# Causal mask added in the maximum, normalisation on ScalarE, and a new plan of the order, in a two-layer transformer block on one core

## The chip, the cores and the metric

The kernel runs on one core of one Trainium2 chip. The metric is the time of the program on the device in microseconds (us); lower is better. A core has five engines that each run their own instructions in order and meet through semaphores: TensorE (PE, matrix products into the banks of PSUM), VectorE (DVE), ScalarE (ACT), GpSimd (POOL) and SyncE (SP), which here issues all DMAs.

## The reference

The input is x of shape (8, 1024, 256), float32: 8 batches of 1024 tokens. Four blocks are applied, each on a layer normalisation of x and added to x:

```
x = x + attention0(norm(x))      16 heads of 16, causal softmax, w_qkv, w_out
x = x + ffn0(norm(x))            entmax-1.5 gates of 16 experts, factored 257 -> 128 -> 1024, exact gelu, back
x = x + attention1(norm(x))      16 heads, projections through a latent of 64, half of each head rotated, causal
x = x + ffn1(norm(x))            squared relu 256 -> 128 -> 256, and routed experts weighted by trunc(prob)
```

norm(x) is (x - mean) / sqrt(var + 1e-5) over 256. In the attentions score[q, k] for k > q is set to minus infinity before the softmax.

## The kernel before

Tokens are worked in halves of a batch, c = 0 or 1, of 512 tokens. `PASSES` (L73 to L80) is the order of the 32 attention passes (batch b, layer l, half c); for each batch from 1 on it is (b, 0, 1), (b-1, 1, 1), (b, 1, 0), (b+1, 0, 0). A pass has four units of four heads (`UNITS`, 128 in all; pass (4, 0, 1) begins with unit 64).

For each unit scores are formed twice. First query by key ("s" items, `score`, L1020): one matmul for each tile of 128 queries, head and part of up to 512 keys, into a ring of three PSUM banks. Where the part ends on the diagonal (2048 of 3072 tiles), a second matmul, identity by `mask_b`, adds -1e30 above the diagonal (L1029). VectorE reduces each tile to its row maximum (`maximum`, L1570). When a unit is through, the maxima are split in three bf16 parts ("mx"), transposed ("mt") and sent by DMA as rows under the queries ("mT"). Then the scores are formed key by query ("st", `scores_t`, L1039, two banks), with the maxima subtracted by those rows; ScalarE takes the exponential (L1336), GpSimd zeroes what lies above the diagonal in the probabilities (`causal`, L1484), and TensorE multiplies them with the values ("pv", L1064, an item for the four heads of a key tile). ScalarE copies the result out ("o"), TensorE transposes it and VectorE divides by the sums ("nm").

Beside the passes run side chains of items. A normalisation (L88) is: statistics on VectorE, the power -1/2 of the variance on GpSimd ("rstd", `inverse_root`, L1453), (x - mean) * rstd on VectorE in two steps of two instructions of 256 columns ("norm", `normalised`, L1537, which waits for GpSimd), and two transposes ("xt"). A projection (L93) has four products "qk" of two matmul pairs each, which ScalarE copies; in layer 1 they are rotated (VectorE "rot", "add", with GpSimd); ScalarE and GpSimd split each in three bf16 parts ("rest", "p1", "p2", GpSimd L1476 and L1481), SP stores the parts (`store_parts`, L842), and later SP loads a unit's stack of queries and keys from there ("ld", `load_stack`, L855, six DMAs). Then come values ("v"). `first_ffn` and `second_ffn` are the other chains.

The order of all items is one list, `ORDER`, made by `program_order` (L397) before the program is built; every engine walks the same list and takes its own items, SP and GpSimd too, so each queue is in the list's order. The planner `Plan` keeps a clock for PE, one busy time for each other engine (`on`, L208, which adds a hop of 0.2 us), and durations in `TIMES` (L145). At each step it lists what could run on PE, each with a time and a rank, and takes the lowest rank among those that can run now, or the earliest. Scores of a unit are "late" (rank 5, else 7) by a line that runs `LEAD` = 7.0 us ahead. `windows` (L172) gives, for every one or two passes, two lists of side steps: chain 0 (outputs and ffn) and chain 1 (loads and projections). They are handed over when the window's first pass begins. Chain 1 has an empty list beside pass (b, 0, 1), `first + ahead` (projections (b, 1, 0) and (b+1, 0, 0)) beside (b-1, 1, 1), and `second` (projections (b+1, 0, 1), then (b, 1, 1)) beside (b, 1, 0) and (b+1, 0, 0). A side chain is "due" (rank 4, else 8) when it lags behind the share of the window that has passed.

## Time and profile before

| | |
|---|---|
| median of 3 runs | 3432.05 us (3427.19 to 3440.59) |
| the profiled execution | 3424.19 us, its span 3422.5 us |
| busy: PE, DVE, ACT, POOL | 3100.3 (91%), 2443.0 (71%), 1927.9 (56%), 1070.7 us (31%) |
| granted clock of TensorE, mean | 0.974 of full speed |
| bytes moved by DMA | 268.54 MB, mean 78 GB/s |

A busy time counts an engine's time once, however many instructions overlap in it; matmuls do overlap, so the duration of one is longer than the time it takes of PE. The granted clock is the share of 2.4 GHz; 0.5 would be its lower level of 1.2 GHz. Durations, waits and chain all come from one execution.

### The profile page before, as it was taken

To read this page: it belongs to the slowest core of one execution; us is meant where nothing else is said; L and a number is where in the kernel's file an instruction comes from. 1 tells how busy PE (TensorE), PEld (TensorE's weight loads), DVE (VectorE), ACT (ScalarE), POOL (GpSimd) and SP (SyncE) were. 2 spreads that over 40 slices of the span, in tenths; PEclk is the share of its full clock that TensorE was granted. 3 is DMA by queue.
4 is the path that set the end of the run, shared out by engine and by line. 5 is a ranking of instruction groups with operands and counts; after the bars stand their busy time and mean duration, and the time that the engine had idled before them with its cause. 6 is when DMAs were issued, how large, how long until landed. Compare 5 with 4: busy or idle time off the path is not lost.

```text
span 3422.5 us, 59720 instructions
## 1 busy us (share of the span) xinstructions
PE 3100.3 (91%) x19319; PEld 1476.2 (43%) x19319; DVE 2443.0 (71%) x6387; ACT 1927.9 (56%) x4092; POOL 1070.7 (31%) x2476
## 2 busy tenths in 40 slices
PE   5899899998999989999899898999989999899997
PEld 3444444444444444434444354444544445344443
DVE  4776686857777577866778567785777847777683
ACT  2456555565465655656556565556655566455654
POOL 2225421345123441324313243132521325213321
PEclk8999999999999999999999999999999999999998
DMA  5415232235222451234413243232442325322240
GB/s 153 105 47 123 65 74 53 65 92 129 50 46 76 107 119 34 58 80 108 102 39 90 56 105 91 56 76 64 108 94 46 81 63 126 66 61 60 57 98 14
DMA packets 241216, 268.54 MB, mean 78 GB/s; under 512 B 19568, under 2 KB 208912, under 8 KB 240912
## 3 DMA queue, kind: packets, MB, share of 16 engines
q1 hardware_dynamic: 240912, 264.66, 32.5%
q8 instruction: 170, 2.79, 0.4%
q14 instruction: 134, 1.10, 0.1%
HBM read 162.35 MB, written 100.66 MB: 77 GB/s over the span
## 4 chain that ended last, share of the span: by engine, by line
PE 60%; DVE 19%; ACT 7%; DMA 6%; issue 4%; SPq 3%; POOL 1%; ACTq 0%; POOLq 0%; DVEq 0%
PE ps L1064 12%; PE ps L1027 10%; PE ps L1047 10%; DVE mx L1573 10%; PE ps L1001 6%; PE ps L993 5%; ACT probs L1336 4%; DMA stk_k<-k 4%; PE ps L1136 3%; PE ps L1131 3%; PE ps L1029 2%; PE ps L1123 2%; PE ps L981 1%; PE ps L1101 1%; DMA stk_q<-mT 1%
## 5 line engine op out<-in xcount | busy, mean ns | idle before, releaser
L1573 DVE TENSOR_REDUCE mx<-ps 128x1 f32<-128x512 f32 (+3 forms) x3072 | 1533.0, 549 | 503.9 <-PE ps L1029 353.5
L1336 ACT ACTIVATE probs<-ps 128x512 f32<-128x512 f32 (+3 forms) x3072 | 1382.2, 491 | 840.9 <-PE ps L1047 820.2
L1490 POOL TENSOR_SCALAR_AFFINE_SELECT probs<-probs 128x128 f32<-128x128 f32 x2048 | 604.9, 305 | 1763.8 <-ACT probs L1336 1734.7
L1027 PE MATMUL ps<-stk_k,stk_q 112*128 112x512 bf16 (+3 forms) x3072 | 882.2, 332 | 124.5 <-DVE mx L1573 69.1
L1047 PE MATMUL ps<-stk_q,stk_k 115*128 115x512 bf16 (+3 forms) x3072 | 893.1, 334 | 78.3 <-ACT probs L1336 47.8
L1064 PE MATMUL ps<-probs,vaug 128*17 128x512 f32 (+3 forms) x6144 | 629.3, 501 | 12.6 <-ACT probs L1336 6.8
L1047 PEld LDWEIGHTS ps<-stk_q,stk_k 115*128 115x128 bf16 x3072 | 273.5, 99 | 604.1 <-ACT probs L1336 419.0
L1027 PEld LDWEIGHTS ps<-stk_k,stk_q 112*128 112x128 bf16 x3072 | 296.1, 98 | 505.9 <-issue 337.5
L1029 PE MATMUL ps<-mask_b,ident_b 128*128 128x128 bf16 x2048 | 440.2, 222 | 0.0
L993 PE MATMUL ps<-turned,wqkv 128*128 128x512 f32 x512 | 265.7, 619 | 3.4 <-ACT turned L1286 1.6
L1029 PEld LDWEIGHTS ps<-mask_b,ident_b 128*128 128x128 bf16 x2048 | 201.5, 98 | 124.8 <-issue 39.6
L1476 POOL TENSOR_TENSOR scratch<-scratch,parts 128x512 f32<-128x512 f32 x128 | 148.1, 1157 | 285.9 <-ACT scratch L1303 264.6
L1064 PEld LDWEIGHTS ps<-probs,vaug 128*17 128x17 f32 x6144 | 121.9, 96 | 244.9 <-issue 109.4
L1286 ACT ACTIVATE turned<-ps 128x512 f32<-128x512 f32 x192 | 112.1, 601 | 127.9 <-PE ps L981 82.7
L1610 DVE TENSOR_TENSOR x<-ps,x 128x512 f32<-128x512 f32 x128 | 88.1, 688 | 126.2 <-PE ps L1001 125.3
L1481 POOL TENSOR_TENSOR parts<-scratch,parts 128x512 bf16<-128x512 f32 x128 | 149.7, 1170 | 46.0 <-ACT parts L1315 46.0
L1351 ACT ACTIVATE scratch<-ps 128x512 f32<-128x512 f32 x128 | 76.4, 597 | 152.5 <-PE ps L1131 152.3
L1131 PE MATMUL ps<-scratch,wout1T 128*128 128x512 f32 x256 | 135.8, 612 | 12.9 <-ACT scratch L1351 12.9
L1001 PE MATMUL ps<-wo,turned 128*128 128x256 f32 x512 | 139.5, 400 | 6.9 <-ACT turned L1286 6.8
L1001 PE MATMUL ps<-wqkv,turned 128*128 128x256 f32 x512 | 135.8, 389 | 0.1
L1136 PE MATMUL ps<-scratch,win 128*128 128x512 f32 x256 | 131.2, 594 | 0.0
L1546 DVE TENSOR_SCALAR xn<-x,mv,rstd 128x256 f32<-128x256 f32 x256 | 98.0, 425 | 40.2 <-POOL rstd L1456 40.2
(145 smaller groups left out, 2646.2 us busy)
## 6 DMA issues: line engine op xcount, KB each, us to landing
k<-parts SPq DMA_DIRECT2D x128, 384.0 KB, 3.4
stk_q<-q SPq DMA_DIRECT2D x256, 192.0 KB, 4.1
stk_k<-k SPq DMA_DIRECT2D x128, 384.0 KB, 6.0
q<-parts SPq DMA_DIRECT2D x64, 384.0 KB, 2.9
stk_k<-k SPq DMA_DIRECT2D x128, 192.0 KB, 4.3
x<-in_L_attn_x SPq DMA_DIRECT2D x16, 512.0 KB, 4.2
k<-parts SPq DMA_DIRECT2D x64, 128.0 KB, 3.4
stk_q<-q SPq DMA_DIRECT2D x128, 64.0 KB, 6.7
```

The costliest lines, as they stand in the source:

```text
L993: ins = pe.matmul(pt, wqkv[l][:, kd, D * w + P * m:D * w + P * (m + 1)], xT(2 * l, b, c, kd), start=kd == 0, stop=kd == KD - 1)
L1001: ins = pe.matmul(pt[:, D * i:D * (i + 1)], left(kd)[:, cols], right(kd), start=kd == 0, stop=kd == n_k - 1)
L1027: ins = pe.matmul(out, q, stk_k[0:ROWS_S, slot, h, BANK * p:BANK * p + width], start=True, stop=not diagonal)
L1029: ins = pe.matmul(out[:, width - P:width], ident_b[:], mask_b[:], start=False, stop=True)
L1047: pe.matmul(st_bank[n % len(ST_BANKS)][:, cols], stk_k[0:ROWS, slot, h, P * j:P * (j + 1)], stk_q[0:ROWS, slot, h, cols], start=True, stop ...
L1064: ins = pe.matmul(o_bank[32 * h:32 * h + DH + 1, cols], vaug[:, v, j % TPC, HG * g + h, :], probs[:, STEP[u, j] % PBUF, h, cols], start=j ...
L1131: pe.matmul(pt, wout1T[:, P * o:P * (o + 1)], z1, start=True, stop=True).then_inc(done, 1)
L1136: pe.matmul(acc, win2[:, k, :], hsb[k % 3], start=k == 0, stop=k == OC - 1)\
L1336: act.activation(probs[:, step % PBUF, h, cols], st_bank[n % len(ST_BANKS)][:, cols], ACT.Exp, scale=SCALE)\
L1481: pool.tensor_tensor(parts[:, o % PRING, 2], qf[o % QRING], parts[:, o % PRING, 1], ALU.subtract)\
L1490: pool.affine_select(out=diag, in_=diag, compare_op=ALU.is_ge, fill=0.0, base=0, pattern=[[1, P]], channel_multiplier=-1).then_inc(p_ready, 1)
L1573: dve.tensor_reduce(mx[:, h, i - TPC * c, p:p + 1], s_bank[n % len(S_BANKS)][:, 0:dict(score_parts(i))[p]], AX.X, ALU.max).then_inc(s_drai ...
```

## The change

- The second matmul of a diagonal tile is gone. VectorE's reduction of such a tile becomes one instruction that adds the last columns of a mask of 512 columns (zero but for the last 128), writes the tile back to PSUM and gives the maximum. The other 1024 tiles are reduced as before.
- "norm" goes from VectorE to ScalarE, as an activation with a per-partition scale (rstd) and bias (shift = -mean * rstd). VectorE computes -mean after the statistics, GpSimd the product after the power. ScalarE waits for it in its own order.
- The planner: other durations, overlap of neighbouring instructions, one transfer queue of all DMAs (`moving`), other ranks, LEAD 9. The waits for a free x slot and for free value slots become steps of the chains. A side chain that is empty takes the next window's list at once (`EARLY`). The ranks were pair 0, mt 1, nm 2, burst 3, due 4, late 5, st 6, s 7, chain 8, single 10 (pair and single are the value products of two key tiles or of one).

```diff
-LEAD = 7.0
+LEAD = 9.0
...
+    old = values_before(b, l, c)
+    if old:
+        steps.append(("after", ("pv", UNIT[old[0], old[1], NG - 1, old[2]], TT - 1)))
...
 def loaded(b, c):
-    return [([("load", b, c)], ""), ([("stat", b, c)], "")]
+    n = NC * b + c - X_SLOTS
+    before = [("after", ("out", n // NC, n % NC))] if n >= 0 else []
+    return before + [([("load", b, c)], ""), ([("stat", b, c)], "")]
...
-    "load": (0.0, ("SP", 6.0)), "stat": (0.0, ("DVE", 2.3)), "rstd": (0.0, ("POOL", 1.0)), "norm": (0.0, ("DVE", 0.9)),
...
-    "rot": (0.0, ("DVE", 1.6), ("POOL", 1.4)), "add": (0.0, ("DVE", 0.75)), "p0": (0.0, ("ACT", 0.6)),
-    "rest": (0.0, ("POOL", 1.25)), "p1": (0.0, ("ACT", 0.6)), "p2": (0.0, ("POOL", 1.25)),
...
-    "logit_": (0.5,), "logit": (0.5, ("DVE", 1.2)), "epow": (0.0, ("POOL", 1.0)), "ent": (0.0, ("DVE", 1.2)),
-    "eroot": (0.0, ("POOL", 1.0)), "at": (0.5, ("ACT", 0.6)), "g": (0.86, ("ACT", 0.6)), "h1_": (0.86,),
...
+    "load": (0.0, ("SP", 6.0)), "stat": (0.0, ("DVE", 2.2)), "rstd": (0.0, ("POOL", 1.35)), "norm": (0.0, ("ACT", 0.8)),
...
+    "rot": (0.0, ("DVE", 1.5), ("POOL", 1.0)), "add": (0.0, ("DVE", 0.68)), "p0": (0.0, ("ACT", 0.63)),
+    "rest": (0.0, ("POOL", 1.16)), "p1": (0.0, ("ACT", 0.63)), "p2": (0.0, ("POOL", 1.16)),
...
+    "logit_": (0.89,), "logit": (0.89, ("DVE", 1.7)), "epow": (0.0, ("POOL", 1.0)), "ent": (0.0, ("DVE", 1.6)),
+    "eroot": (0.0, ("POOL", 1.0)), "at": (0.44, ("ACT", 0.6)), "g": (1.05, ("ACT", 0.6)), "h1_": (0.86,),
...
-        self.busy[engine] = max(self.busy[engine], start) + time
-        return self.busy[engine] + HOP
+        begin = max(self.busy[engine], start)
+        self.busy[engine] = begin + time - OVERLAP[engine]
+        return begin + time + SEEN
+    def transfer(self, start, number, time):
+        begin = max(self.busy["SP"], start)
+        self.busy["SP"] = begin + 0.5 * number + 0.1
+        self.moving = max(self.moving, begin + 1.3) + time
+        return max(self.moving, begin + 1.5) + 0.3
...
-                self.parts[item[1:]] = self.on("SP", time, 1.2) + 2.5
+                self.parts[item[1:]] = self.transfer(time, 3.6 if item[5] else 1, 2.2 if item[5] == 0 else 5.3)
...
-            self.loads[u] = self.on("SP", start, 6 * 0.6) + 3.0
+            self.loads[u] = self.transfer(start, 6, 7.9 if UNITS[u][3] else 5.3)
...
+        self.pe = max(self.pe, self.score_time()) + width / 2400 + 0.003
-        self.pe = max(self.pe, self.score_time()) + width / 2300 + (0.09 if diagonal else 0.02)
-        end = self.on("DVE", self.pe + HOP, 0.12 + width / 1000)
+        end = self.on("DVE", self.pe + HOP, (0.2 if diagonal else 0.15) + width / 960)
...
-        self.rows[u] = self.on("SP", end, 0.6) + 2.2
+        self.rows[u] = self.transfer(end, 1.4, 0.1)
...
-        self.pe = max(self.pe, self.scores_t_time(u, j, h)) + (z - a) / 2300
-        end = self.on("ACT", self.pe + HOP, 0.04 + (z - a) / 1000)
+        self.pe = max(self.pe, self.scores_t_time(u, j, h)) + (z - a) / 2400 + 0.003
+        end = self.on("ACT", self.pe + HOP, 0.17 + (z - a) / 1200)
...
-            end = self.on("POOL", end, 0.32)
+            end = self.on("POOL", end, 0.29)
...
-        self.pe = start + 4 * (z - a) / 2400 + 0.2
+        self.pe = start + 4 * (z - a) / 2400 + 0.02 + (0.2 if alone else 0.1)
...
-        if todo and (not main or position >= window_end):
-            passes, *beside = todo.pop(0)
-            for n in range(2):
-                plan.chains[n] += beside[n]
-            for step in beside[1]:
-                if step[0] != "after" and step[0] and step[0][0][0] == "qk_" and step[1]:
-                    for w in range(2):
-                        plan.chains[2 + w] += splits(*step[0][0][1:4], w)
+        begin = todo and (not main or position >= window_end)
+        for n in range(2):
+            if todo and (begin or EARLY and not plan.chains[n]):
+                beside, todo[0][1 + n] = todo[0][1 + n], []
+                plan.chains[n] += beside
+                for step in beside:
+                    if step[0] != "after" and step[0] and step[0][0][0] == "qk_" and step[1]:
+                        for w in range(2):
+                            plan.chains[2 + w] += splits(*step[0][0][1:4], w)
+        if begin:
+            passes = todo.pop(0)[0]
...
+RANK = dict(mt=1, nm=2, burst=3, late=4, st=5, pair=5.5, due=6, s=7, chain=8, single=10)
+EARLY = True
...
-                diagonal = BANK * p + width == P * (i + 1)
                 q = stk_q[0:ROWS_S, slot, h, P * i - BANK * c:P * (i + 1) - BANK * c]
-                ins = pe.matmul(out, q, stk_k[0:ROWS_S, slot, h, BANK * p:BANK * p + width], start=True, stop=not diagonal)
-                if diagonal:
-                    ins = pe.matmul(out[:, width - P:width], ident_b[:], mask_b[:], start=False, stop=True)
-                ins.then_inc(s_full, 1)
+                pe.matmul(out, q, stk_k[0:ROWS_S, slot, h, BANK * p:BANK * p + width], start=True, stop=True).then_inc(s_full, 1)
...
+            def normalised(n, b, c, a):
+                i, src = NC * n + c, x[:, x_slot(b, c)]
+                if a == 0:
+                    act.wait_ge(ln_rstd, LN["rstd", n, b, c] + 1)
+                    if normed:
+                        bk, k = PLACE["xt", *normed[-1], KD - 1]
+                        act.wait_ge(full[bk], k + 1)
+                    normed.append((n, b, c))
+                for t in range(2 * a, 2 * a + 2):
+                    ins = act.activation(xn[:, t, :], src[:, t, :], ACT.Identity, bias=shift[:, i, t:t + 1], scale=rstd[:, i, t:t + 1])
+                ins.then_inc(xn_ready, 1)
...
-                pool.tensor_tensor(rstd[:, i], veps[:, i], neg_half[:], ALU.pow).then_inc(ln_rstd, 1)
+                pool.tensor_tensor(rstd[:, i], veps[:, i], neg_half[:], ALU.pow).then_inc(ln_root, 1)
+                pool.wait_ge(ln_root, LN["rstd", n, b, c] + 1)
+                pool.tensor_tensor(shift[:, i], minus[:, i], rstd[:, i], ALU.mult).then_inc(ln_rstd, 1)
...
+                dve.tensor_scalar(minus[:, i], mv[:, i, :, 0], -1.0, None, ALU.mult)
...
-                dve.tensor_reduce(mx[:, h, i - TPC * c, p:p + 1], s_bank[n % len(S_BANKS)][:, 0:dict(score_parts(i))[p]],
-                                  AX.X, ALU.max).then_inc(s_drained, 1)
+                width = dict(score_parts(i))[p]
+                tile, top = s_bank[n % len(S_BANKS)][:, 0:width], mx[:, h, i - TPC * c, p:p + 1]
+                if BANK * p + width == P * (i + 1):
+                    dve.tensor_tensor_reduce(tile, tile, mask_b[:, BANK - width:BANK], 1.0, LOWEST, ALU.add, ALU.max, top)\
+                        .then_inc(s_drained, 1)
+                else:
+                    dve.tensor_reduce(top, tile, AX.X, ALU.max).then_inc(s_drained, 1)
```

## Rows read from the trace of the kernel before

**Rows 1.** Page, part 1: busy us (share of span) xinstructions, by engine.
```profile
PE 3100.3 (91%) x19319; PEld 1476.2 (43%) x19319; DVE 2443.0 (71%) x6387; ACT 1927.9 (56%) x4092; POOL 1070.7 (31%) x2476
```

**Rows 2.** Page, part 4: chain that ended last, share of the span by engine, by line.
```profile
PE 60%; DVE 19%; ACT 7%; DMA 6%; issue 4%; SPq 3%; POOL 1%; ACTq 0%; POOLq 0%; DVEq 0%
PE ps L1064 12%; PE ps L1027 10%; PE ps L1047 10%; DVE mx L1573 10%; PE ps L1001 6%; PE ps L993 5%; ACT probs L1336 4%; DMA stk_k<-k 4%; PE ps L1136 3%; PE ps L1131 3%; PE ps L1029 2%; PE ps L1123 2%; PE ps L981 1%; PE ps L1101 1%; DMA stk_q<-mT 1%
```

**Rows 3.** Windows: us, busy us (xinstructions) of each engine, PEclk, DMA share, GB/s.
```profile
0.00:70.00 70.00, 34.53 (x170) 22.00 (x170) 28.12 (x42) 17.75 (x30) 12.88 (x22) 0.87 0.42 132
3360.00:3422.50 62.50, 39.47 (x184) 19.40 (x184) 10.65 (x37) 19.89 (x44) 6.84 (x22) 0.74 0.05 18
```

**Rows 4.** Waits of the whole run: who <- for whom: us, times, longest us.
```profile
DVE mx L1573 <- PE ps L1029: 353.5, 316, 8.8
...
PE ps L1027 <- DVE mx L1573: 69.1, 141, 2.6
...
PE ps L1047 <- ACT probs L1336: 47.8, 135, 1.2
...
PE ps L1027 <- DMA stk_k<-k: 45.9, 29, 3.9
...
PE ps L1047 <- DMA stk_q<-mT: 19.7, 7, 3.9
```

**Rows 5.** Windows, six stretches: the one at 2070, and all six summed.
```profile
2070.00:2110.00 40.00, 31.59 (x231) 13.41 (x223) 32.40 (x73) 17.35 (x41) 14.68 (x40) 0.91 0.64 138
...
sum 245.00, PE 196.93 PEld 84.60 DVE 196.60 ACT 109.78 POOL 93.70; mean PE 32.82 PEld 14.10 DVE 32.77 ACT 18.30 POOL 15.62
```

**Rows 6.** Chain of waits, 1625 to 1700: start us, us, what.
```profile
1649.45 1.14 POOL parts L1481
1650.60 0.56 SPq L852
...
1657.22 7.49 DMA stk_k<-k
...
1688.98 6.01 DMA stk_q<-mT
```

**Rows 7.** Timeline of TensorE: start us, us, engine, line, instruction.
```profile
1646.06 0.22 PE L1027 MATMUL ps<-stk_k,stk_q 112*128 112x128 bf16 x1
1646.12 0.22 PE L1029 MATMUL ps<-mask_b,ident_b 128*128 128x128 bf16 x1
1646.17 0.22 PE L1027 MATMUL ps<-stk_k,stk_q 112*128 112x128 bf16 x1
```

**Rows 8.** Page, part 5: group | busy us, mean ns | idle before, releaser.
```profile
L1573 DVE TENSOR_REDUCE mx<-ps 128x1 f32<-128x512 f32 (+3 forms) x3072 | 1533.0, 549 | 503.9 <-PE ps L1029 353.5
```

**Rows 9.** Groups by line and shape, VectorE: | busy us, mean ns | idle before.
```profile
L1573 DVE TENSOR_REDUCE mx<-ps 128x1 f32<-128x512 f32 x1536 | 1008.1, 682 | 241.1 <-PE ps L1027 136.7 <-PE ps L1029 98.3
...
L1610 DVE TENSOR_TENSOR x<-ps,x 128x512 f32<-128x512 f32 x128 | 88.1, 688 | 126.2 <-PE ps L1001 125.3
...
L1695 DVE SCALAR_TENSOR_TENSOR scratch<-ps,bias,scratch 128x512 f32<-128x512 f32 x32 | 24.0, 750 | 13.6 <-PE ps L1123 8.6 <-PE ps L1136 5.0
```

**Rows 10.** The same view, all engines: normalisation and the rows near its new form.
```profile
L1546 DVE TENSOR_SCALAR xn<-x,mv,rstd 128x256 f32<-128x256 f32 x256 | 98.0, 425 | 40.2 <-POOL rstd L1456 40.2
...
L1533 DVE TENSOR_SCALAR veps<-mv 128x4 f32<-128x4 f32 x64 | 11.5, 179 | 2.2
...
L1336 ACT ACTIVATE probs<-ps 128x512 f32<-128x512 f32 x1536 | 856.8, 598 | 417.3 <-PE ps L1047 409.6
...
L1336 ACT ACTIVATE probs<-ps 128x256 f32<-128x256 f32 x512 | 184.0, 383 | 137.6 <-PE ps L1047 131.4
...
L1315 ACT ACTIVATE parts<-scratch 128x512 bf16<-128x512 f32 x128 | 81.3, 635 | 25.1 <-POOL scratch L1476 25.1
...
L1490 POOL TENSOR_SCALAR_AFFINE_SELECT probs<-probs 128x128 f32<-128x128 f32 x2048 | 604.9, 305 | 1763.8 <-ACT probs L1336 1734.7
...
L1456 POOL TENSOR_TENSOR rstd<-veps,neg_half 128x4 f32<-128x4 f32 x64 | 64.6, 1009 | 63.6 <-DVE veps L1533 63.6
```

More of the change, by code:

```diff
@@ L82, with values_before @@
 UNIT = {key: u for u, key in enumerate(UNITS)}
+X_SLOTS = 5
+def values_before(b, l, c):
+    if c == l == 0:
+        return (b - 1, 0, 1) if b > 1 else None
+    if c == l:
+        return (b - 1, 1, 1) if b else (0, 0, 1)
+    if l:
+        return (b, 0, 1) if b else None
+    return (b - 2, 1, 1) if b > 1 else (0, 0, 1) if b else None
 def normalisation(n, b, c):
@@ L154 @@
-    "keep": (0.0,), "route_": (0.5,), "route": (0.5, ("DVE", 0.9)), "up_": (0.86,), "up": (0.86, ("ACT", 0.6), ("DVE", 0.8)),
-    "gate": (0.0, ("ACT", 0.3), ("DVE", 1.3)), "down": (0.9, ("DVE", 0.7)), "out": (0.0,),
-}
+    "load": (0.0, ("SP", 6.0)), "stat": (0.0, ("DVE", 2.2)), "rstd": (0.0, ("POOL", 1.35)), "norm": (0.0, ("ACT", 0.8)),
+    "xt": (0.44, ("ACT", 0.6)), "yt": (0.44, ("ACT", 0.6)), "qk_": (0.86,), "qk": (0.86, ("ACT", 0.9)),
+    "rot": (0.0, ("DVE", 1.5), ("POOL", 1.0)), "add": (0.0, ("DVE", 0.68)), "p0": (0.0, ("ACT", 0.63)),
@@ new lines @@
+    "rest": (0.0, ("POOL", 1.16)), "p1": (0.0, ("ACT", 0.63)), "p2": (0.0, ("POOL", 1.16)),
+    "v_": (0.86,), "v": (0.86, ("ACT", 0.6)), "ao_": (0.86,), "ao": (0.86, ("DVE", 1.9)),
+    "logit_": (0.89,), "logit": (0.89, ("DVE", 1.7)), "epow": (0.0, ("POOL", 1.0)), "ent": (0.0, ("DVE", 1.6)),
+    "eroot": (0.0, ("POOL", 1.0)), "at": (0.44, ("ACT", 0.6)), "g": (1.05, ("ACT", 0.6)), "h1_": (0.86,),
+    "h1": (0.86, ("DVE", 0.75)), "hid": (0.86, ("ACT", 0.6)), "z": (0.86,), "fo": (0.86, ("DVE", 1.9)),
@@ L157 @@
+    "keep": (0.0,), "route_": (0.89,), "route": (0.89, ("DVE", 1.1)), "up_": (0.86,), "up": (0.86, ("ACT", 0.6), ("DVE", 0.75)),
+    "gate": (0.0, ("ACT", 0.3), ("DVE", 1.6)), "down": (0.86, ("DVE", 0.7)), "out": (0.0,),
+}
+OVERLAP = {"ACT": 0.1, "DVE": 0.08, "POOL": 0.0, "SP": 0.0}
+SEEN = 0.06
 HOP = 0.2
@@ L199, in __init__ @@
         self.free, self.turn, self.ring, self.st, self.steps, self.pvs, self.held = [0.0, 0.0], 0, [], [], {}, [], []
-        self.parts, self.rows, self.out = {}, {}, {}
+        self.parts, self.rows, self.out, self.moving = {}, {}, {}, 0.0
         self.s_unit, self.s_items, self.waiting, self.outputs, self.s_first, self.loads = 0, score_items(0), [], [], {}, {}
@@ L359, in weigh_pair, with weigh @@
     def weigh_pair(self):
-        self.weigh()
-        self.weigh()
-    def weigh(self):
+        self.weigh(False)
+        self.weigh(False)
+    def weigh(self, alone=True):
         u, j = self.held[0]
@@ L404, in program_order @@
         total += DENSE * unit_work(u)
-    todo = windows()
+    todo = [list(window) for window in windows()]
     window_end = 0
@@ L476, in program_order @@
                 if time < NEVER:
-                    choices.append((time, 3 if burst else 4 if due else 8, "chain", (n,)))
+                    choices.append((time, RANK['burst'] if burst else RANK['due'] if due else RANK['chain'], "chain", (n,)))
         time = plan.score_time()
         if time is not None:
-            choices.append((time, 5 if late(plan.s_unit, len(plan.s_items)) > 0 else 7, plan.score, ()))
+            choices.append((time, RANK['late'] if late(plan.s_unit, len(plan.s_items)) > 0 else RANK['s'], plan.score, ()))
         if main and "gelu" not in plan.locks and position < window_end:
@@ L483, in program_order @@
             if time is not None:
-                choices.append((time, 6, "st", main[0]))
+                choices.append((time, RANK['st'], "st", main[0]))
         if not choices:
```

47 lines of the change are left out of this document (13 added, 34 removed).

## The prediction

> **What bounds the kernel now.** I read the page's busy shares first: TensorE (PE) 3100.3 of 3422.5 us, and in the table VectorE (DVE) at 2443.0, ScalarE (ACT) at 1927.9, GpSimd (POOL) at 1070.7 [rows 1]. The reader is to see one engine nearly full and a second at seven tenths. Next the chain that ended last: 60% of it is PE, 19% DVE, 7% ACT, 9% transfers and their issue (DMA 6%, SPq 3%), 4% issue [rows 2]. So an edit on PE is worth most of what it takes away, one on DVE about a quarter: 19% of 3422.5 is 650 us of chain on 2443 us of busy time, or 27%.
>
> Then PE's idle time, 3422.5 - 3100.3 = 322 us. Start (0 to 70) and end (3360 on) hold 59 of it, in which no edit does much: 70 - 34.53 = 35.5, and 62.5 - 39.47 = 23 [rows 3]. Of the rest the list of waits names 69.1 us behind VectorE's maxima, 47.8 behind exponentials, and 45.9 and 19.7 behind the transfers of a stack and of the row maxima [rows 4]. These transfer waits are not spread out. Six stretches of 40 to 45 us, one per batch, hold a hole in PE: the one shown has 31.59 busy of 40 at a granted clock of 0.91 in place of 1.00, and all six 196.9 of 245, so 48 us idle [rows 5]. The chain through the one at 1650 tells why: the split of a projection on POOL ends at 1650.6, only then SP sends its stores (L852) and, behind them in its in-order queue, the load of the next stack; that takes 7.49 us; then the row maxima take 6.01 us more, and PE has transposed scores again at 1688.98 + 6.01 = 1695.0 [rows 6]. That the load stands behind these stores follows from the order of items: unit 64's "ld" comes after the "p2" of (3, 1, 1, 0, 1). The planner had written that load 3.6 us of SP and 3.0 us of landing, and the projection's split at times of its own.
>
> **The change, part by part.** All sums are made against the profiled execution (3424.2 us, span 3422.5). The median of the runs shown is 3432.05, so I add 8 us at the end.
>
> (A) Mask off TensorE. 2048 matmuls of 128 columns and their weight loads go. A row says 219 ns for one, but that is a latency. What one takes of PE's time is start to start, from the mask to the next score: 1646.12 to 1646.17, and 0.06 from the score to the mask where the score has as many columns, so 0.06 us [rows 7]; 2048 x 0.06 = 123 us. That is the upper bound (PE counts everywhere). The lower is the share of line L1029 in the chain, 2% or 68 us [rows 2]. I take 85: above the chain's share because a score tile also reaches DVE a step earlier, and DVE's longest wait is for L1029 (353.5 us) [rows 4]. Saved: **85 (68 to 123)**.
>
> (B) Mask on VectorE. In the 2048 diagonal tiles of the 3072, a reduction becomes add, maximum and a write of the tile back to PSUM. No row shows this instruction. At width 512 the reduction takes 682 ns, a tensor-tensor add with one operand in PSUM 688, a three-operand one out of PSUM 750 [rows 9]. So +6 to +68 ns, 12 to 139 us of DVE. If the maximum is delivered by a small instruction of its own, a row of 4 elements of 179 ns [rows 10] bounds it: 367 us. I take +0.05, 102 us, near the upper of the two 512-wide rows, since this one must both write the tile and deliver a value. L1573 is 10% of the chain [rows 2], 342 us, on 1533 us busy [rows 8], so 22% of it is on the path: 102 x 0.22 = 22 us. Lost: **22 (3 to 81)**. A doubling is a rival below. DVE also loses the reason to wait for the second matmul.
>
> (C) Normalisation on ScalarE. DVE gives up 256 instructions of 425 ns, 98.0 us of work [rows 10], and gets 64 small ones of 179 ns, 11.5 us. ScalarE gets 256 of 256 columns. Its rows: 383 ns for 256 columns out of PSUM, 635 for 512 from SBUF [rows 10]; those are the ends, 98 to 163 us. The slope (598 - 383)/256 = 0.84 ns taken off the SBUF row gives 0.42 us, so 108 us. POOL gets 64 products of 4 columns between 305 ns (its mask of the probabilities) and 1009 (its power), 20 to 65 us, and each normalisation starts that much later [rows 10]. On the path: DVE gives back 86 x 0.27 = 23; ACT, whose 7% of the chain is 240 us on 1928 busy (12%), takes 108 x 0.12 = 13; the later start costs between nothing and all 65, and I put it at 5, since POOL has 1% of the chain [rows 2]. Saved: **5 (-62 to +11)**; the ends are 23 - 20 - 65 and 23 - 12. Queued behind the new wait on ScalarE are the exponentials; behind the old one on DVE were the maxima.
> The Trainium skill (ScalarE: Activation LUTs, section What ACT_TABLE_LOAD costs) puts 186 ns + 0.833 ns per element on an activation with immediates and about 93 more for each per-partition operand, of which there are two here: 585 ns, 150 us in all. By it ScalarE would take 18 us of path in place of 13. No row here has such an operand.
>
> (D) The hole per batch. Three edits aim at it. The planner now carries one transfer queue with 7.9 us for a stack of the second half. LEAD goes from 7 to 9, so scores run further ahead. And an empty side chain takes its next window's steps at once: beside pass (b, 0, 1) the second chain's list is empty in every batch from 1 on, so the projections for layer 1 and the next batch can start there, a window before they do now, and the splits on POOL are done before the stack load stands behind their stores. If they work, the six holes give 48 us and the clock up to 9% of 245, 22: 70 at most. What is late next is DVE, 32.40 of 40 busy there already [rows 5], and it must do the same maxima. I take **40 (0 to 70)**.
>
> (E) The rest of the order. 322 - 59 - 48 = 215 us of PE idle remain, of which 69.1 + 47.8 are waits for DVE and ACT of 0.35 to 0.5 us in the mean (47.8/135, 69.1/141) [rows 4], the size of the corrections in the new table (0.02 to 0.5 us an item). The ranks change too: pairs of value products no longer go first, side chains that are due go behind scores. It can cut either way: two thirds of the 117 named, or half the 69 on top. I take **20 (-35 to +80)**.
>
> Sum: -85 + 22 - 5 - 40 - 20 = -128; 3424 - 128 = 3296, plus 8: 3304, rounded to **3300 us**.
>
> **The rivals.**
> 1. The order pays fully (chance 0.15). PE becomes the only bound: 123 of (A), 70 of (D), 60 of (E), less 22 for (B) and 20 of new waits on ScalarE: 3424 - 211 + 8 = about 3220. For it: 215 us of idle are in waits that a true model can see. Against it: where PE is short of work now DVE is at 80% [rows 5], and no order removes maxima.
> 2. The order gives nothing (0.17): (D) and (E) at zero, because the holes only move to another place or the early projections compete with work that was ready. Then 3424 - 68 + 8 = 3364. For it: the load is in SP's queue behind stores whatever the planner believes, and POOL runs 93.7 us of the 245 there [rows 5].
> 3. ScalarE's new wait gives the gain back (0.08), the case on the other side. The place is the first of two normalising steps: ScalarE stands in order until POOL has power and product (1.0 + 0.3 to 1.0 us) and then works 4 x 0.42 = 1.7 us, while two banks of transposed scores cover 2 x 0.6 = 1.2 us. If it always arrives too early, PE loses up to 2.5 us for each of 64 normalisations, 160 us: 3296 + 160 + 8 = 3464. It decides from 2 us per normalisation (128/64). For it: PE waits for the exponentials in 135 places already [rows 4]. Against it: DVE, which had this wait, stood in it 40.2 us in all [rows 10].
> 4. VectorE's new instruction runs at half rate (0.05). The reduction's time per element is (682 - 549)/(512 - 384) = 1.04 ns, 384 being the mean width of all 3072 [rows 8, 9]; once more of it is 333 ns at the diagonal tiles' mean width of 320, 681 us of DVE: 2443 - 86 + 681 = 3038 us, over PE's 2977. At the 0.91 that the fullest engine now reaches this is 3340; if a second pass takes the whole of a 688 ns add (0.49 us at width 320, 1000 us), 3357/0.91 = 3690. It decides from 0.37 us per tile (3424 x 0.91 = 3116, less 2357, over 2048).
> The Trainium skill (Vector Engine (DVE) Microarchitecture Reference, section 7, Points that are easy to get wrong) says that such a form with two non-bf16 SBUF sources runs at half throughput. By that rule it would be the 3340, but here one source is in PSUM and the mask is bf16.
>
> **How the numbers follow.** Forecast 0.55, with its own range 3255 to 3345. The terms' bounds give 3432 - 123 + 3 - 11 - 70 - 80 = 3151 and 3432 - 68 + 81 + 62 + 35 = 3542, which don't meet in one run. Leaving out about one in ten on each side, with rival 1 inside and rival 2 inside: **3215 to 3390**. A measurement of this kernel can tell about 0.5%, 17 us. Faster: 0.55 + 0.15 + 0.17 and half of rival 4 less what their edges lose, 0.86; within 0.5%: 0.05; slower: 0.09, from rivals 3 and 4.
>
> **What would show it.** (A) No row of the mask on PE, PE busy about 2980 to 3010. (B) The new DVE row at width 512 in 690 to 790 ns; above 1000, rival 4. (C) Normalising rows on ScalarE of 0.38 to 0.6 us; its wait for POOL under 60 us in all; over 120, rival 3. (D) In the list of waits, PE behind stack and row-maxima transfers down from 65.6 us to under 25; if it stays, rival 2. (E) PE idle under 270 us. The prediction is wrong if PE's busy share falls below 0.88: then the time sits in waits that I take for cured.

## The result and the profile after

The changed kernel takes 3278.31 us (median of 4 runs, 3268.96 to 3287.42) against 3429.62 of the kernel before, timed beside it: ratio 0.9558, 95% interval 0.9512 to 0.9604. Forecast were 3300 us and a range of 3215 to 3390. The profiled execution took 3268.96 us, span 3267.1, so 155 us less than before.

Page of the changed kernel, part 1, busy time by engine, to be laid beside [rows 1]:
```profile
PE 2958.2 (91%) x17271; PEld 1344.2 (41%) x17271; DVE 2447.2 (75%) x8243; ACT 2018.0 (62%) x4348; POOL 1082.0 (33%) x2540
```
TensorE's busy time fell by 142 us, its idle time only from 322 to 309. Part 4, the chain, beside [rows 2]:
```profile
PE 57%; DVE 22%; ACT 10%; issue 4%; DMA 3%; POOL 2%; SPq 2%; ACTq 0%; DVEq 0%; POOLq 0%
PE ps L1083 11%; PE ps L1066 11%; PE ps L1049 10%; PE ps L1024 6%; DVE ps L1599 6%; ACT probs L1369 5%; DVE mx L1602 4%; PE ps L1016 4%; PE ps L1155 3%; PE ps L1150 3%; ACT xn L1318 2%; PE ps L1004 2%; DMA stk_k<-k 1%; PE ps L1142 1%; PE ps L1091 1%
```
TensorE went from 60 to 57%, VectorE from 19 to 22%, ScalarE from 7 to 10%, transfers and SP from 9 to 5%. Waits (who <- for whom: us, times, longest), beside [rows 4]:
```profile
PE ps L1066 <- ACT probs L1369: 52.4, 136, 1.4
...
PE ps L1049 <- DVE mx L1599: 41.0, 95, 9.6
...
PE ps L1049 <- DVE mx L1602: 17.9, 72, 0.7
...
PE ps L1066 <- DMA stk_q<-mT: 13.1, 25, 1.1
```
```profile
PE ps L1049 <- DMA stk_k<-k: 2.1, 4, 0.7
```
The transfer waits of TensorE went from 65.6 to 15.2 us: the holes at the stack loads are gone. On these lines the waits for maxima (69.1 before, 58.9 now) and for exponentials (47.8, now 52.4) stayed. Summed over all lines of TensorE that wait for maxima they are 85.6 before and 94.3 now. The new instructions, groups by line and shape, beside [rows 9, 10]:
```profile
L1602 DVE TENSOR_REDUCE mx<-ps 128x1 f32<-128x512 f32 x1024 | 702.0, 686 | 112.9 <-PE ps L1049 109.0 <-DVE hq L1755 0.2
L1599 DVE CUSTOM_DVE_ANT_0 ps<-ps,mask_b 128x512 f32<-128x512 f32 x512 | 347.7, 699 | 111.4 <-PE ps L1049 109.5
L1599 DVE DVE_READ_ACCUMULATOR2_ANT mx<- 128x1 f32 x2048 | 286.4, 140 | 0.0
...
L1599 DVE CUSTOM_DVE_ANT_0 ps<-ps,mask_b 128x128 f32<-128x128 f32 x512 | 145.5, 303 | 42.1 <-PE ps L1049 41.2
```
```profile
L1318 ACT ACTIVATE xn<-x,shift,rstd 128x256 f32<-128x256 f32 x256 | 138.7, 598 | 56.3 <-POOL shift L1493 55.6
```
```profile
L1493 POOL TENSOR_TENSOR shift<-minus,rstd 128x4 f32<-128x4 f32 x64 | 12.9, 201 | 5.0
```
The masked maximum is two instructions, 699 ns at width 512 and 140 ns for the read of the accumulator. The timeline shows what the pair takes:
```profile
1569.92 0.73 DVE L1599 CUSTOM_DVE_ANT_0 ps<-ps,mask_b 128x512 f32<-128x512 f32 x1
1570.57 0.14 DVE L1599 DVE_READ_ACCUMULATOR2_ANT mx<- 128x1 f32 x1
1570.57 0.73 DVE L1599 CUSTOM_DVE_ANT_0 ps<-ps,mask_b 128x512 f32<-128x512 f32 x1
...
1571.22 0.73 DVE L1599 CUSTOM_DVE_ANT_0 ps<-ps,mask_b 128x512 f32<-128x512 f32 x1
```
Start to start it is 0.65 us, since the next instruction begins together with the read. The plain reduction of the same width, back to back, starts every 0.60 us in the trace of the kernel before. A normalising row on ScalarE takes 598 ns where I had put 420; the product on GpSimd takes 201 ns.

### The profile page after: what moved, and what is told of

It is laid out like the page before. It is cut to its first block, busy times and chain, and to the rows that moved or that the text cites. A ratio compares the mean times of both kernels' runs of the same rounds, so it can differ in the third digit from the quotient of the medians.

```text
span 3267.1 us, 57797 instructions
## 1 busy us (share of the span) xinstructions
PE 2958.2 (91%) x17271; PEld 1344.2 (41%) x17271; DVE 2447.2 (75%) x8243; ACT 2018.0 (62%) x4348; POOL 1082.0 (33%) x2540
## 4 chain that ended last, share of the span: by engine, by line
PE 57%; DVE 22%; ACT 10%; issue 4%; DMA 3%; POOL 2%; SPq 2%; ACTq 0%; DVEq 0%; POOLq 0%
PE ps L1083 11%; PE ps L1066 11%; PE ps L1049 10%; PE ps L1024 6%; DVE ps L1599 6%; ACT probs L1369 5%; DVE mx L1602 4%; PE ps L1016 4%; PE ps L1155 3%; PE ps L1150 3%; ACT xn L1318 2%; PE ps L1004 2%; DMA stk_k<-k 1%; PE ps L1142 1%; PE ps L1091 1%
## 5 line engine op out<-in xcount | busy, mean ns | idle before, releaser
L1599 DVE CUSTOM_DVE_ANT_0 ps<-ps,mask_b 128x512 f32<-128x512 f32 (+3 forms) x2048 | 978.0, 503 | 278.6 <-PE ps L1049 271.7
L1066 PE MATMUL ps<-stk_q,stk_k 115*128 115x512 bf16 (+3 forms) x3072 | 876.8, 331 | 82.5 <-ACT probs L1369 52.4
L1049 PE MATMUL ps<-stk_k,stk_q 112*128 112x512 bf16 (+3 forms) x3072 | 845.0, 330 | 80.3 <-DVE mx L1599 41.0
L1602 DVE TENSOR_REDUCE mx<-ps 128x1 f32<-128x512 f32 x1024 | 702.0, 686 | 112.9 <-PE ps L1049 109.0
L1083 PE MATMUL ps<-probs,vaug 128*17 128x512 f32 (+3 forms) x6144 | 615.8, 493 | 19.4 <-POOL probs L1527 10.3
L1049 PEld LDWEIGHTS ps<-stk_k,stk_q 112*128 112x128 bf16 x3072 | 287.0, 98 | 567.9 <-issue 452.2
L1599 DVE DVE_READ_ACCUMULATOR2_ANT mx<- 128x1 f32 x2048 | 286.4, 140 | 0.0
L1318 ACT ACTIVATE xn<-x,shift,rstd 128x256 f32<-128x256 f32 x256 | 138.7, 598 | 56.3 <-POOL shift L1493 55.6
L1630 DVE RECIPROCAL rec<-ps 128x16 f32<-128x16 f32 x128 | 32.9, 257 | 172.4 <-PE ps L1091 162.1
```

Of the source, the lines that this page charges most:

```text
L1049: pe.matmul(out, q, stk_k[0:ROWS_S, slot, h, BANK * p:BANK * p + width], start=True, stop=True).then_inc(s_full, 1)
L1066: pe.matmul(st_bank[n % len(ST_BANKS)][:, cols], stk_k[0:ROWS, slot, h, P * j:P * (j + 1)], stk_q[0:ROWS, slot, h, cols], start=True, stop ...
L1083: ins = pe.matmul(o_bank[32 * h:32 * h + DH + 1, cols], vaug[:, v, j % TPC, HG * g + h, :], probs[:, STEP[u, j] % PBUF, h, cols], start=j ...
L1318: ins = act.activation(xn[:, t, :], src[:, t, :], ACT.Identity, bias=shift[:, i, t:t + 1], scale=rstd[:, i, t:t + 1])
L1599: dve.tensor_tensor_reduce(tile, tile, mask_b[:, BANK - width:BANK], 1.0, LOWEST, ALU.add, ALU.max, top)\
L1602: dve.tensor_reduce(top, tile, AX.X, ALU.max).then_inc(s_drained, 1)
```

## The experiments

Ratios are to the kernel before, timed beside each run, with their 95% intervals. Differences in microseconds are differences of ratios times 3430; one against the changed kernel carries its interval, 16 us to either side, and those of the others besides. First the three parts, one by one: mask (M), normalisation (N), order (O).

**M alone, and M without VectorE's price.** The first run has the mask's part of the change and nothing else; `ORDER` is the old one, item for item. The second leaves the mask out of these scores altogether:

```diff
-                if diagonal:
-                    ins = pe.matmul(out[:, width - P:width], ident_b[:], mask_b[:], start=False, stop=True)
...
+                    dve.tensor_tensor_reduce(tile, tile, mask_b[:, BANK - width:BANK], 1.0, LOWEST, ALU.add, ALU.max, top)\
+                        .then_inc(s_drained, 1)
```
and for the second, on top of it:
```diff
-                if BANK * p + width == P * (i + 1):
-                    dve.tensor_tensor_reduce(tile, tile, mask_b[:, BANK - width:BANK], 1.0, LOWEST, ALU.add, ALU.max, top)\
-                        .then_inc(s_drained, 1)
-                else:
-                    dve.tensor_reduce(top, tile, AX.X, ALU.max).then_inc(s_drained, 1)
+                dve.tensor_reduce(top, tile, AX.X, ALU.max).then_inc(s_drained, 1)
```

> Only the mask is moved from TensorE to VectorE's maximum; normalisation stays on VectorE, and the order of items is the old one, item for item. Theory A (steps A and B of the prediction: 85 us saved, 22 lost): ratio to before 0.982, some 3368 us; PE busy down by 120 to 140 us, but PE idle up by 60, because the old order leaves PE waiting for VectorE. Rival (most of the whole gain is this edit, since in the trace of after TensorE's busy time fell by 142 us and its idle time by only 13): ratio 0.965, some 3310 us, PE idle up by less than 20 us.

> The old order and normalisation on VectorE, and no mask in the query-by-key scores at all: the mask matmuls are gone and VectorE reduces every tile as before, so the row maxima are taken over the whole diagonal tile. They are then upper bounds of the causal maxima; any bound gives the same softmax, and the probabilities above the diagonal are still zeroed by GpSimd. So it is the mask-only run less VectorE's extra work. Theory (VectorE's add and accumulator read, 71 us of busy time there, took back what TensorE saved): ratio to before 0.975 to 0.982, 50 to 75 us better than the mask-only run. Rival (in the old order TensorE's mask time lay beside waits anyway): within 15 us of the mask-only run, ratio 0.993 or more.

Measured: M alone 3422.65 us, ratio 0.9976 (0.9962 to 0.9990). Without VectorE's price 3408.68 us, 0.9927 (0.9906 to 0.9948). In microseconds that is 8 and 25: in the old order VectorE's add cost 17, and taking the mask matmuls off TensorE, 123 us by the prediction's estimate, was worth 25. The first run fell outside both its theories; of their signs only the idle time (up by 60 foretold, 55 measured) held. In the second the theory fell and the rival was all but met: 14 us by the medians and 17 by the ratios, where it said 15, and 0.9927 where it said 0.993. Page, part 1, of M alone, then of the run without the mask:
```profile
PE 3041.6 (89%) x17271; PEld 1341.2 (39%) x17271; DVE 2514.1 (74%) x8435; ACT 1925.3 (56%) x4092; POOL 1070.2 (31%) x2476
```
```profile
PE 3044.8 (89%) x17271; PEld 1347.7 (40%) x17271; DVE 2440.9 (72%) x6387; ACT 1924.0 (56%) x4092; POOL 1071.2 (31%) x2476
```
In both TensorE's busy time falls by 56 to 59 us, not by 123, and its idle time, span less busy, rises from 322 to 377 and 367. Its waits in M alone:
```profile
PE ps L1032 <- DVE mx L1578: 65.7, 162, 3.0
PE ps L1049 <- ACT probs L1338: 54.6, 155, 1.4
PE ps L1032 <- DMA stk_k<-k: 49.5, 36, 3.2
PE ps L1032 <- DVE mx L1581: 31.7, 66, 1.6
```
Maxima 97.4 in place of 69.1, exponentials 54.6 for 47.8, the stack's transfer 49.5 for 45.9. TensorE comes sooner to the same waits. And its granted clock fell, from 0.974 to:
```profile
core 0: 3418.8 us, clock 0.965
```
On 3042 us of busy time that is 28 us at most. The start times of the matmuls close the account. In the kernel before, the step from a mask matmul to the next matmul is 0.058 or 0.059 us for over six in ten of the 2048 and longer for the rest; at 0.058 that makes 119 us in all. Of these, 55 came back as idle time. Busy time fell by only 59, so another 60 came back inside it: some 28 as a lower clock at most, the rest as longer steps from one matmul to the next. What they waited for no row tells. VectorE's 17 us are within these sums.

**N in the old order.** On top of M:

```diff
-                    ins = dve.tensor_scalar(xn[:, t, :], src[:, t, :], mv[:, i, t, 0:1], rstd[:, i, t:t + 1],
-                                            ALU.subtract, ALU.mult)
...
+                    ins = act.activation(xn[:, t, :], src[:, t, :], ACT.Identity, bias=shift[:, i, t:t + 1], scale=rstd[:, i, t:t + 1])
```

> Mask on VectorE and normalisation on ScalarE, with the old order. Theory (step C, 5 us saved): within 0.3% of the mask alone. Rival (ScalarE's 598 ns per normalising instruction and its wait for GpSimd delay exponentials in an order that was not planned for it): 0.5 to 1.5% slower than the mask alone, with ScalarE's wait for the shift over 60 us.

Measured: 3424.01 us, 0.9972 (0.9957 to 0.9987): no change against M alone. The theory (within 0.3% of M alone) stood and the rival fell; ScalarE waited 22.4 us for the shift, where the rival wanted over 60.

**O alone, and N and M in the new order.** The order of the changed kernel with the old work, then with N, with M, and (the changed kernel) with both. The first has the diff of the planner alone; the other two undo one part of the changed kernel:

```diff
-                    dve.tensor_tensor_reduce(tile, tile, mask_b[:, BANK - width:BANK], 1.0, LOWEST, ALU.add, ALU.max, top)\
...
+                    ins = pe.matmul(out[:, width - P:width], ident_b[:], mask_b[:, BANK - P:BANK], start=False, stop=True)
```
```diff
-                    ins = act.activation(xn[:, t, :], src[:, t, :], ACT.Identity, bias=shift[:, i, t:t + 1], scale=rstd[:, i, t:t + 1])
...
+                    ins = dve.tensor_scalar(xn[:, t, :], src[:, t, :], mv[:, i, t, 0:1], rstd[:, i, t:t + 1],
+                                            ALU.subtract, ALU.mult)
```

> The new order of items with the old work: mask matmuls on TensorE, normalisation on VectorE. Theory (steps D and E, 60 us saved): ratio to before 0.982. Rival 1 (the order only pays with the new work, for which its durations are made): ratio 1.00. Rival 2 (the holes at the stack loads are all that it cures): ratio 0.987, PE's idle time behind transfers of stack and row maxima under 25 us here too.

> The changed kernel with the mask matmuls back on TensorE (its order and its normalisation on ScalarE unchanged). Theory (TensorE's time is worth nearly all of itself in the new order, since its chain share of PE is still 57%): 85 to 123 us slower than the changed kernel less 22 given back by VectorE, so ratio to before 0.975 to 0.985. Rival (under the new order VectorE bounds and the mask is free on TensorE): ratio 0.960 or less.

> The changed kernel with normalisation back on VectorE, everything else and the order item for item the same: VectorE then has both the mask and the normalisation. Theory (VectorE's time has a price in the new order that it has not in the old: moving normalisation off it was worth 37 us there with the mask on TensorE): 37 to 60 us slower than the changed kernel, ratio to before 0.966 to 0.973. Rival (those 37 us were GpSimd's and ScalarE's timing, not VectorE's load, so they don't grow and the mask still pays its 43): 3310 to 3320 us, ratio 0.964 to 0.967. Second rival (VectorE overloaded, so the mask pays nothing without the other move): 3345 us or more, ratio 0.974 or more.

| | old order | new order |
|---|---|---|
| old work | 1 | 0.9782 (0.9759 to 0.9805) |
| N | not run | 0.9673 (0.9652 to 0.9694) |
| M | 0.9976 (0.9962 to 0.9990) | 0.9700 (0.9679 to 0.9721) |
| M and N | 0.9972 (0.9957 to 0.9987) | 0.9558 (0.9512 to 0.9604) |
| N, no mask in these scores | not run | 0.9503 (0.9478 to 0.9529) |

The medians were 3358.43 (order alone), 3321.38 (with N), 3328.28 us (with M). In microseconds the order alone gives 75, N on top of it 37, M on top of that 39; the other way round M 28 and then N 49. In the old order M and N together give 10. And taking the mask matmuls away with no price on VectorE is worth 58 us in the new order (0.9673 to 0.9503, normalisation on ScalarE in both), 25 in the old. The order alone came close to its theory (0.982) and far from rival 1. Rival 2 had the transfer waits right, 15.4 us with the old work too, but not the size, 0.987. With the mask back on TensorE the ratio, 0.9673, fell between its two cases, 0.975 and 0.960: the mask was worth 39 us, not the 63 to 101 of the theory. Part 1 of the mask back on TensorE, and of the changed kernel with normalisation back on VectorE:
```profile
PE 3056.7 (92%) x19319; PEld 1483.4 (45%) x19319; DVE 2378.9 (72%) x6195; ACT 2023.0 (61%) x4348; POOL 1081.6 (33%) x2540
```
```profile
PE 2997.2 (90%) x17271; PEld 1359.7 (41%) x17271; DVE 2517.8 (75%) x8435; ACT 1905.3 (57%) x4092; POOL 1072.1 (32%) x2476
```
From the first to the changed kernel busy falls by 98.5 us and idle rises by 43. The second was 49 us slower than the changed kernel, within the 37 to 60 of its theory, with 30% of the chain on VectorE where the changed kernel has 22%. But it does not show the theory's price. Its rival said that the 37 us would not grow, and 37 and 49 differ by less than their intervals. And 81 us less of VectorE, in the maxima, were worth only 19 in the same order (the run without the mask, below), or 23%; at that price the 71 us of normalisation would be worth 17. The contrast between 49 and 19 is not clear of noise either, since both are measured against the changed kernel. That the mask still pays 28 speaks against the second rival.

What stands beside it is another wait: TensorE's transposes (L1004) wait for the normalised rows. In order: the order alone, the old work with its own plan (below), the changed kernel with normalisation back on VectorE, the changed kernel:
```profile
PE ps L1004 <- DVE xn L1569: 36.1, 19, 4.7
```
```profile
PE ps L1004 <- DVE xn L1569: 15.3, 8, 4.7
```
```profile
PE ps L1004 <- DVE xn L1565: 40.1, 19, 4.7
```
```profile
PE ps L1004 <- ACT xn L1318: 18.1, 15, 5.7
```
With the mask on TensorE and normalisation on ScalarE it is 19.1 us; in the old order it is 15.4 with normalisation on VectorE and 14.9 on ScalarE, where the move was worth nothing. So 17 of the 37 us and 22 of the 49 lie in this wait, and it is long only where an order that was planned for normalisation on ScalarE runs it on VectorE. Maxima are the next part: summed over all lines, TensorE waits 81.4 us for them in the order alone and 66.1 with N, 117.1 and 94.3 in the other pair. The trace with normalisation back on VectorE is of an execution 16 us above the median of its kernel, so these differences are somewhat too large.

**What in the order.** Three runs of the changed kernel, each with one part of its planner taken back.

```diff
-EARLY = True
+EARLY = False
```
```diff
-RANK = dict(mt=1, nm=2, burst=3, late=4, st=5, pair=5.5, due=6, s=7, chain=8, single=10)
+RANK = dict(pair=0, mt=1, nm=2, burst=3, due=4, late=5, st=6, s=7, chain=8, single=10)
```
```diff
-            self.loads[u] = self.transfer(start, 6, 7.9 if UNITS[u][3] else 5.3)
+            self.loads[u] = self.on("SP", start, 6 * 0.6) + 3.0
...
```

The third takes back all durations, hops and the transfer queue.

> The changed kernel, planned with EARLY = False: a side chain gets its next list only when its window begins. Theory (the early start is what removes the stack-load holes, step D, 40 us): 30 to 50 us slower than the changed kernel, ratio to before 0.966 to 0.970, and PE's waits for the transfer of a stack back above 30 us. Rival (truer durations alone remove them): within 10 us of the changed kernel, ratio 0.958, those waits under 10 us.

> The changed kernel, planned with the old ranks (pairs of value products first, due side chains before late scores and transposed scores). Theory (step E, 20 us in all, ranks the larger part): 10 to 20 us slower than the changed kernel, ratio 0.960 to 0.963. Rival (ranks are the core of the order's gain, because VectorE's maxima are what PE must keep fed): 50 us or more slower, ratio 0.971 or more, with VectorE's wait for scores up by over 50 us.

> The changed kernel, planned with the old durations, hops and transfers, but with the new ranks, LEAD 9 and the early start. Theory (the transfer model is what sees the holes): 20 to 40 us slower than the changed kernel, ratio 0.963 to 0.969. Rival (durations hardly matter, the rules do): within 10 us, ratio under 0.959.

Measured: without the early start 3319.86 us, 0.9664 (0.9638 to 0.9689), 36 us worse than the changed kernel; old ranks 3376.87, 0.9838 (0.9814 to 0.9861), 96 worse; old durations 3328.97, 0.9689 (0.9667 to 0.9712), 45 worse. Together that is 177, more than the 142 that the whole new order gives on top of M and N (0.9972 to 0.9558). That the parts need each other is likely but not clear of noise, since the changed kernel's interval enters the first sum three times. LEAD and the chains' new waits for free slots had no run of their own. Waits for transfers, without the early start and then with the old durations:
```profile
PE ps L1049 <- DMA stk_k<-k: 7.2, 8, 4.2
...
PE ps L1066 <- DMA stk_q<-mT: 3.7, 7, 0.6
```
```profile
PE ps L1049 <- DMA stk_k<-k: 44.7, 25, 4.0
...
PE ps L1066 <- DMA stk_q<-mT: 20.3, 11, 3.5
```
and with the old ranks:
```profile
PE ps L1049 <- DMA stk_k<-k: 27.3, 15, 3.7
```
With 7.0 us for row maxima that is 34.3. The 65 us of transfer waits come back whole with the old durations, in part with the old ranks, and not without the early start (10.9). So the durations with the transfer queue closed the holes, with help of the ranks. For the early start the theory had the size and its rival the transfer waits; for the ranks the rival (50 us or more) stood; for the durations the ratio lay at the edge of the theory, 0.969. The early start earns its 36 us elsewhere. Where, the page of each run shows; without the early start, then with the old ranks:
```profile
PE 3005.9 (91%) x17271; PEld 1354.9 (41%) x17271; DVE 2449.3 (74%) x8243; ACT 2022.7 (61%) x4348; POOL 1080.9 (33%) x2540
```
```profile
PE 3048.7 (90%) x17271; PEld 1342.5 (40%) x17271; DVE 2422.7 (72%) x8243; ACT 2026.0 (60%) x4348; POOL 1083.9 (32%) x2540
```
The changed kernel and these two have the same 17271 matmuls, and yet TensorE is busy 2958, 3006 and 3049 us. Their granted clocks, 0.981, 0.972 and 0.969, explain 27 and 36 of the 48 and 91 us if all busy time goes with the mean clock. Split by the granted clock, TensorE's busy time at 2.4 GHz is 2861, 2852 and 2867 us in the three traces, and at 1.2 GHz 97, 154 and 182 us. So the extra busy time lies nearly all in stretches at the lower level. If all that is busy there is work at half rate, the lower clock explains half of what was added there, 29 and 42 us. This is an estimate; the rest, 19 and 48 us, are then longer steps from one matmul to the next, since the matmuls are the same. How a wait can hide there is argued: a row of 0.22 us of which 0.06 is its turn [rows 7] covers a wait of 0.16 behind it. What these steps waited for is not shown. Idle time differs little (309, 311 and 323 us), though waits move within it: without the early start TensorE waits 83.5 us for exponentials in place of 57.3, and 69.2 for maxima in place of 94.3. VectorE waits longer for scores in both, 377.7 us without the early start and 405.8 with the old ranks, where it was 271.7:
```profile
DVE ps L1599 <- PE ps L1049: 405.8, 319, 30.2
```

**The planner for the old work.**

```diff
-    "rstd": (0.0, ("POOL", 1.35)), "norm": (0.0, ("ACT", 0.8)),
+    "rstd": (0.0, ("POOL", 1.0)), "norm": (0.0, ("DVE", 0.8)),
...
-        self.pe = max(self.pe, self.score_time()) + width / 2400 + 0.003
-        end = self.on("DVE", self.pe + HOP, (0.2 if diagonal else 0.15) + width / 960)
+        self.pe = max(self.pe, self.score_time()) + width / 2400 + (0.06 if diagonal else 0.003)
+        end = self.on("DVE", self.pe + HOP, 0.15 + width / 960)
```

> The work of before (mask matmuls on TensorE, normalisation on VectorE) with the new planner, whose durations are set to that work: 0.06 us of PE per mask, 0.15 us + width/960 of VectorE for every maximum, normalisation 0.8 us on VectorE, power 1.0 us on GpSimd. Theory 1 (the order of the changed kernel was bad for the old work only because it was planned for other work): better than the order-only run by 15 us or more, ratio to before 0.974 or less. Theory 2 (the planner's rules carry the gain whatever the work): within 8 us of the order-only run, ratio 0.976 to 0.981.

Measured: 3340.64 us, 0.9730 (0.9709 to 0.9752), 18 us better than the order alone (3358.43). Theory 1 stands, a little above its 15 us (the intervals leave 7 to 29), and the wait for the normalised rows, 36.1 us in the order alone and 15.3 here, is 21 us shorter. Of the whole gain of 151 us 93 are then to be had with no change of the work, and mask and normalisation together are worth the other 59.

**Better than both.**

> The changed kernel without the mask in the query-by-key scores (maxima over the whole diagonal tile, one reduction of the old kind), with its order item for item. Theory (VectorE's 90 us of extra busy time at the 22% to 30% that VectorE has of the chain): 20 to 30 us better than the changed kernel, ratio to before 0.947 to 0.950. Rival (VectorE bounds in the scores' stretches): 50 us or more better, ratio under 0.941.

> The same work as the run before it (no mask in those scores, normalisation on ScalarE), with every maximum at 0.15 us + width/960 in the planner, and ranks, LEAD, PACE, DENSE and SPREAD set by a random search that minimised the planner's own finish. It finishes 95 us earlier by the planner's clock than with the ranks of the changed kernel. Theory (the planner's differences hold on the chip, as the 50 us for the early start came out as 41): 60 to 95 us better than the run before it, ratio to before 0.920 to 0.932. Rival (the search fits the planner's errors): less than 30 us better, ratio 0.940 or more.

The first is the edit shown above for the old order. The second's, in the planner alone:

```diff
-        end = self.on("DVE", self.pe + HOP, (0.2 if diagonal else 0.15) + width / 960)
+        end = self.on("DVE", self.pe + HOP, 0.15 + width / 960)
...
-LEAD = 9.0
-PACE = 0.9
-DENSE = 2.0
-SPREAD = 1.0
+LEAD = 14.9
+PACE = 0.64
+DENSE = 2.3
+SPREAD = 1.78
...
-RANK = dict(mt=1, nm=2, burst=3, late=4, st=5, pair=5.5, due=6, s=7, chain=8, single=10)
+RANK = dict(mt=0.0, nm=5.3, burst=0.7, late=4.4, st=3.7, pair=5.5, due=5.5, s=9.7, chain=6.3, single=10)
```

Measured: 3258.89 us, 0.9503 (0.9478 to 0.9529), and 3248.89 us, 0.9465 (0.9440 to 0.9491). The first is 19 us better than the changed kernel, just under the stated 20 to 30, on 81 us less of VectorE; its rival (50 or more) fell. The searched order gave 10 of the 95 us that the planner saw, so its rival (less than 30) stood; the intervals of the two overlap. Part 1 of the page and the clock, first of the run without the mask, then of the searched order:
```profile
PE 2959.0 (91%) x17271; PEld 1351.1 (41%) x17271; DVE 2365.9 (73%) x6195; ACT 2018.9 (62%) x4348; POOL 1084.8 (33%) x2540
```
```profile
core 0: 3256.6 us, clock 0.977
```
```profile
PE 2976.4 (92%) x17271; PEld 1359.4 (42%) x17271; DVE 2367.3 (73%) x6195; ACT 2014.8 (62%) x4348; POOL 1082.6 (33%) x2540
```
```profile
core 0: 3247.4 us, clock 0.964
```
Idle time fell from 298 to 271 us, but the granted clock from 0.977 to 0.964 of full speed, which on 2959 us of busy time is 39 us. Busy time at 1.2 GHz rose from 117 to 205 us, half of which rise is 44. Given back whole, these would bring the 10 us to 54 at most, still under the 60 to 95 foretold: the lower clock took a part, and the planner was too hopeful besides. How the two share it stays open. These two kernels rest on maxima over keys that the mask excludes; with scores much larger above the diagonal than below, exponentials could vanish, so it suits data like these.

## Why the prediction came out right, and where it was wrong

**What bounds, and the sum.** 3424 - 128 + 8 = 3304 was forecast, 3278 measured. But the terms are not those of the sum, and that the total came so close is partly luck, as the last paragraph shows.

**(A) and (B), mask, 85 saved and 22 lost: mis-sized.** The mask's net worth is 8 us in the old order, 28 or 39 in the new. Wrong was the lower bound: the 68 us of L1029 in the chain [rows 2] were taken for a floor, and the full removal gave 25 in the order that this share was read from. A chain's share is what it holds now; when it goes, the wait that had lain beside it takes its place, here the maxima, the exponentials and the transfers. The upper bound was read well: by the start times of all masks it is 119 us, not 123. TensorE's busy time, foretold as 2980 to 3010, came out at 2958. VectorE's term was near: I took 50 ns a tile and 22 us; busy time grew by 35 to 40 ns a tile (2514.1 less 2443.0, and 2447.2 less 2365.9, over 2048), and it cost 17 us in the old order and 19 in the new, the second with the changed kernel's interval of 16. The rival of half rate fell: rows of 699 ns at width 512 and 303 at width 128 give one element per 1.03 ns, as the plain reduction has [rows 8, 9], not half of that. The rule of the Trainium skill (Vector Engine (DVE) Microarchitecture Reference, section 7, Points that are easy to get wrong) is on two non-bf16 sources in SBUF; here one was in PSUM and the mask was bf16, so no run here tests it.

**(C), normalisation, 5 saved: mis-sized, and my duration wrong.** It was worth 37 to 49 us in the new order and nothing in the old. The ScalarE row is 598 ns; the estimate of 585 ns worked out from the Trainium skill's figures (ScalarE: Activation LUTs, What ACT_TABLE_LOAD costs) was within 3% of it, and my 420, a slope taken off rows without such operands, was not. That did not matter much, since ScalarE has room: with nothing else changed its busy time rose by 113 to 116 us. The sum priced the 86 us off VectorE at 27%. They measured 71 to 74, and the maxima's time was worth 23% in both orders, so the price was fair as far as these runs tell. What it left out is the way from the normalised rows to TensorE: I had counted the later start on GpSimd, but not TensorE's wait for the rows, 36 and 40 us in the new order with normalisation on VectorE and 18 to 19 without. What the other half of the 37 to 49 is stays open.

**(D), 40 saved: the size of the effect right, the cause wrong in part.** The transfer waits fell by 50 us as said. But of the edits named it was the truer transfers in the planner, not the early start, and the new ranks, counted under (E), had 19 us of it (34.3 us of waits with the old ones, 15.2 without). What the closed holes alone are worth in time no run separates.

**(E), 20 saved: too small.** The ranks alone are worth 96 us with the rest in place. I had looked for them in TensorE's idle time, 215 us, and put the sign that idle would be under 270; it is 309. They came out of busy time, 91 us of it, by the estimate above 42 through the clock.

**The order as a whole** was put at 60 and gave 75 alone. So errors cancelled: forecast were 63 for the mask, 5 for normalisation and 60 for the order; measured, in the sequence order, N, M, were 39, 37 and 75. The 24 too many for the mask stood against 32 too few for normalisation and 15 for the order. Rival 3 fell: ScalarE stood 55.6 us behind GpSimd, under the 60 that I had set, and TensorE 18.1 us behind the normalised rows. Rival 2 fell with the order-only run, rival 1 by 58 us, and rival 4 by the rows of (B).

## What to carry to other kernels

Where an order is written out by hand or by a planner, the price of an engine's time depends on the order: some 120 us of matmuls were worth 25 us under the old one and 58 under one made for the lighter work, so replan before an edit is judged, and run the 2 x 2. A share of the chain is no lower bound for what its removal gives; ask what stands beside each instance. Nor is an engine's share a price for every edit on it: in one order 81 us off VectorE in the maxima gave 19, and 71 us off it in normalisation gave 49, where TensorE's wait for the moved work's result fell by 22 (19 and 49 are not clear of noise against each other, the wait is read from the traces). So look at who waits for the result. Idle time does not hold all of an engine's waiting: the same 17271 matmuls were 2958 us busy in one order and 3049 in another, with 97 and 182 us of it at the lower clock.

## What the runs showed of the hardware

- The add-and-maximum with an output in PSUM took 0.65 us from start to start at width 512; with its accumulator read (140 ns, most of it overlapped) it costs 35 to 40 ns more of busy time than a plain reduction, whose starts lie 0.60 us apart at this width. From width 128 to 512 both go at one element per 1.03 to 1.04 ns.
- An activation with scale and bias read per partition took 598 ns for 256 columns from SBUF; one of 256 columns out of PSUM with constants 383 [rows 10].
- TensorE's mean granted clock was 0.981 in the changed kernel's profile, and 0.960 to 0.965 in five others with the same matmuls (M alone, M and N in the old order, no mask in the old order, the old durations, the searched order). Over all their executions the ranges are 0.975 to 0.981 and 0.960 to 0.970. Four of these have more idle time than the changed kernel (332 to 378 us in place of 309), the fifth less than any other with these matmuls, 271; so idle time alone does not tell the clock.
- The clock differs between executions of one kernel: the changed kernel took 3269 and 3270 us at 0.981, and 3286 and 3287 us at 0.975 and 0.976.
